# Macaron block (MoE, attention, MoE) on one core: attention output with tokens on partitions, layer 1's router begun inside the last attention steps, and two expert loads moved

## Chip, cores and metric

One core of a Trainium2 chip runs the whole program in one launch. The metric is the device time of that launch in microseconds (us). Engines: PE is TensorE, DVE is VectorE, ACT is ScalarE, POOL is GpSimd, SP is SyncE, which here only issues DMAs.

## What is computed

x has 8 x 256 = 2048 tokens of D = 256, float32. Two mixture-of-experts layers stand around one attention layer:

```python
x = x + 0.5 * moe(layernorm(x), router_w, w1, v1, w2)      # E = 64 experts, top K = 8, F = 96
x = x + attention(layernorm(x), Wq, bq, Wk, bk, Wv, bv, Wo, bo)  # H = 16 heads of 128, KV = 4
x = x + 0.5 * moe(layernorm(x), router_w, w1, v1, w2)

# moe: rows of tokens in order (position, batch); each expert keeps its first C = 32 tokens
probs = softmax(x @ router_w.T); wts, idx = top_k(probs, 8); wts = wts / sum(wts)
h = silu(xg @ w1) * (xg @ v1); y = h @ w2                  # xg: the 32 tokens of each expert
out[token] += weight * y
# attention: grouped queries, softmax(Q K^T / sqrt(128)) V per head, then @ Wo + bo
```

## The kernel before

**Layout.** x stays on chip as `x[128, 16, 256]`, token on partition, 16 tiles of 128 tokens. All engines run hand-written programs that meet at semaphores. PE, DVE, ACT and POOL each run theirs in order, so the order of the code is the order of the work.

**MoE layer.** PE transposes the token tiles (`transpose_tokens(layer, u)`, two tiles each, into PSUM bank u % 2), multiplies by the router (`experts_of`) and transposes the logits back (`logits_of`); ACT copies each result (`copy_tokens`, `copy_expert_major`, `copy_logits`). DVE takes the top eight of each token in four `masks(layer, n)` of four tiles each, with small operations of the layer norm (`moment_steps`) in between. PE packs the masks into codes (line 1338), DVE finds the first 32 tokens of each expert (`expert_layer` of DVE, lines 920 to 942), PE moves them to slots (line 1347, the slot product), and POOL gathers token rows from a table in DRAM by indirect DMA (line 552), one DMA for each of 16 groups of four experts. At most five gathers are in flight ahead. PE then walks the 16 groups (`slot_step`): transpose of the slots (line 1189), up product (1257), down product (1267), and one-hot products that sum into PSUM banks 5 to 7 (1201, 1217), which `take_tokens` has filled with x before (lines 1231 for 64 tokens of a tile, 1236 for 16 more). `keep_busy(n)` (line 1225) issues n matmuls whose result nobody uses; each shows as two in the profile, since a float32 matmul runs in two passes.

**Expert weights.** Group g needs 768 KB (up) and 512 KB (down). Homes for them share memory with other tensors: `q` (4 homes, over Wq, Wk, Wv), `r` (4, over attention's tensors), `o` (3, over Wo), `s` (1, over router tensors), and `r` again for groups 12 to 15. SP's program is one queue: in layer 1 it loads groups 0 to 3 during the last block of attention, 4 and 5 when attention is done, writes the token table (`store_table`), waits for two gathers, then loads 6 to 11, then 12 to 15 as homes come free. In layer 0, groups 4 to 11 follow the table at once, then 12 to 15, and behind them Wk, Wq, Wv, Wo.

**Attention.** Four blocks of 512 tokens (two sequences). Float32 products are made of three float32r products of high and low parts (`three`, lines 1406 to 1408). ACT takes the high part out of PSUM, DVE the low part (`take_high`, `take_low`), in two work banks used in turn; `work()` waits until the use before last was taken. A block has 16 steps, `place(n)` gives kv head, sequence bb and pair of heads hp. In `step(n)` of PE stand, in this order: scores of n+1, transposes of the probabilities of n, the first projection (`fills`: q each step, k in every fourth, xT and v near the block's end), the output products that are due, further projections, and the P·V product of n into a work bank, whose low part is o_lo. DVE's `step(n)`: maxima of n+1, probsT_lo, first projection, normalisation of probs n+1, other projections, o_lo, statistics (line 1150).

**Output.** `out_ps[d]` (banks 6 and 7) holds the output transposed: 128 columns of D on partitions, 512 tokens. In the first block up to step 12 `output_product` does one step: 12 matmuls of 256 columns. Later `output_of_pair` does two steps of a pair with one d at once: 6 matmuls of 512 columns. When a block is done ACT adds the bias on the way out (`take_output`, line 733), PE transposes it back (`transpose_output`, line 1506, in steps 2 and 3 of the next block, each in a work bank; `output`, line 1517, at the end), and DVE adds it to x (`add_output`, line 1103; `last_output`, line 1112):

```python
ps = work()
for t in range(4):
    last = nc.tensor.transpose(ps[:, t * P:t * P + P], yT[:, d, t * P:t * P + P], ident[:])
last.then_inc(y_ready, 1)
```

**From attention to layer 1.** The last step (15) already transposes tokens of tiles 0 to 3. Then, on PE: experts_of(1,0), tokens 2 and 3 (tiles 4 to 7), logits, last output product, experts 1, tokens 4 and 5, `output()`, and the rest. DVE does masks 0 with the moments of 12 tiles, the last add, its statistics, then masks 1 to 3.

## Time and profile before

| | us |
|---|---|
| median of 3 runs | 665.5 (663.27 to 667.88) |
| the profiled execution | 667.9 |
| its span, first to last instruction | 666.0 |
| PE busy | 626.7 |
| DVE busy | 498.3 |
| ACT busy | 391.1 |
| POOL busy | 52.4 |

The profile is of one execution, 2.4 us above the median. Busy times of PE overlap, since matmuls are pipelined: a matmul's duration is from its start to its modelled end, and the pace is read from the starts. PEclk is the share of full clock that TensorE was granted, 1.00 for 2.4 GHz, 0.50 for 1.2 GHz. In a timeline row "[0.48 <-DVE q_lo L1073]" means that the engine had been idle for 0.48 us until line 1073 released it.

### The profile page before, as it was taken

To read this page: it belongs to the slowest core of one execution; us is meant where nothing else is said; L and a number is where in the kernel's file an instruction comes from. 1 tells how busy PE (TensorE), PEld (TensorE's weight loads), DVE (VectorE), ACT (ScalarE), POOL (GpSimd) and SP (SyncE) were. 2 spreads that over 40 slices of the span, in tenths; PEclk is the share of its full clock that TensorE was granted. 3 is DMA by queue.
4 is the path that set the end of the run, shared out by engine and by line. 5 is a ranking of instruction groups with operands and counts; after the bars stand their busy time and mean duration, and the time that the engine had idled before them with its cause. 6 is when DMAs were issued, how large, how long until landed. Compare 5 with 4: busy or idle time off the path is not lost.

```text
span 666.0 us, 11671 instructions
## 1 busy us (share of the span) xinstructions
PE 626.7 (94%) x4320; PEld 525.8 (79%) x4320; DVE 498.3 (75%) x1309; ACT 391.1 (59%) x1053; POOL 52.4 (8%) x75
## 2 busy tenths in 40 slices
PE   8589999999999999999999999999999999887995
PEld 6367677999888888888888888888888888665774
DVE  6746668889988677887777788876778877773663
ACT  5634475767666566566556666666666656662441
POOL 3443000000000000000000000000000000134210
PEclk9689999999999999999999999999999999969998
DMA  8999940000000000000000000000000034266991
GB/s 318 341 416 419 376 153 1 2 1 1 0 1 1 1 1 0 1 1 1 0 1 1 1 0 1 1 1 0 1 1 2 0 127 190 110 207 228 419 376 48
DMA packets 27619, 62.50 MB, mean 94 GB/s; under 512 B 7014, under 2 KB 17382, under 8 KB 27558
## 3 DMA queue, kind: packets, MB, share of 16 engines
q1 hardware_dynamic: 25398, 55.97, 22.2%
q0 software_dynamic: 1664, 5.30, 2.1%
q8 instruction: 37, 0.61, 0.4%
q10 hardware_dynamic: 496, 0.43, 0.3%
q14 instruction: 24, 0.20, 0.1%
HBM read 54.34 MB, written 7.34 MB: 93 GB/s over the span
## 4 chain that ended last, share of the span: by engine, by line
PE 72%; DVE 12%; ACT 6%; DMA 6%; issue 2%; POOL 1%; SPq 0%; POOLq 0%; DVEq 0%; ACTq 0%
PE bank L1406 18%; PE bank L1408 17%; PE bank L1407 17%; PE bank L1462 7%; PE bank L1217 3%; DMA slots<-token_table,slot_index 3%; DMA down_r<-down_in 3%; PE bank L1257 2%; ACT probs L728 2%; PE bank L1225 2%; PE bank L1267 2%; ACT probsT_hi L739 1%; DVE q_lo L1073 1%; ACT q_hi L711 1%; DVE probsT_lo L1129 1%
## 5 line engine op out<-in xcount | busy, mean ns | idle before, releaser
L728 ACT ACTIVATE probs<-bank,negmax 128x256 f32<-128x256 f32 x256 | 121.4, 494 | 1.8 <-DVE negmax L1087 1.6
L739 ACT CAST probsT_hi<-bank 128x512 fp32r<-128x512 f32 x128 | 68.8, 590 | 70.9 <-PE bank L1462 70.9
L711 ACT ACTIVATE o_hi<-bank,bv 128x512 fp32r<-128x512 f32 x64 | 44.1, 690 | 69.2 <-PE bank L1408 69.2
L1129 DVE TENSOR_TENSOR probsT_lo<-bank,probsT_hi 128x512 fp32r<-128x512 f32 x128 | 81.7, 679 | 0.4 <-ACT probsT_hi L739 0.4
L1087 DVE TENSOR_REDUCE negmax<-bank 128x2 f32<-128x512 f32 x128 | 81.7, 679 | 0.0
L1095 DVE TENSOR_SCALAR probs<-probs,rowinv 128x256 f32<-128x256 f32 x256 | 73.0, 348 | 2.3
L1073 DVE SCALAR_TENSOR_TENSOR o_lo<-bank,bv,o_hi 128x512 fp32r<-128x512 f32 x64 | 48.0, 749 | 34.5 <-ACT o_hi L711 34.5
L1408 PE MATMUL bank<-k_hi,q_lo 128*128 128x256 f32 x256 | 72.4, 283 | 0.0
L1407 PE MATMUL bank<-k_lo,q_hi 128*128 128x256 f32 x256 | 72.3, 283 | 0.0
L1406 PE MATMUL bank<-k_hi,q_hi 128*128 128x256 f32 x256 | 72.2, 282 | 0.0
L1073 DVE SCALAR_TENSOR_TENSOR q_lo<-bank,bq,q_hi 128x512 fp32r<-128x512 f32 x64 | 47.9, 748 | 32.2 <-ACT q_hi L711 31.9
L1462 PE MATMUL bank<-ident,probs 128*128 128x128 f32 x512 | 66.4, 273 | 0.6 <-DVE probs L1095 0.6
L1462 PEld LDWEIGHTS bank<-ident,probs 128*128 128x128 f32 x512 | 57.3, 140 | 1.1 <-DVE probs L1095 1.1
L1406 PE MATMUL bank<-probsT_hi,v_hi 128*128 128x512 f32 x128 | 52.0, 406 | 6.1 <-DVE q_lo L1073 4.1
L728 ACT ACTIVATION_READ_ACCUMULATOR probs<-bank,negmax 128x1 f32 x256 | 57.6, 225 | 0.0
L1406 PE MATMUL bank<-o_hi,wo_hi 128*128 128x512 f32 (+1 forms) x160 | 56.6, 354 | 0.0
L1408 PE MATMUL bank<-o_hi,wo_lo 128*128 128x512 f32 (+1 forms) x160 | 55.7, 348 | 0.0
L1407 PE MATMUL bank<-o_lo,wo_hi 128*128 128x512 f32 (+1 forms) x160 | 55.4, 346 | 0.0
L1406 PE MATMUL bank<-xT_hi,wq_hi 128*128 128x512 f32 x128 | 54.3, 424 | 0.2 <-DVE k_lo L1073 0.2
L711 ACT ACTIVATE q_hi<-bank,bq 128x512 fp32r<-128x512 f32 x64 | 44.9, 702 | 15.0 <-PE bank L1408 15.0
L1406 PEld LDWEIGHTS bank<-k_hi,q_hi 128*128 128x128 f32 x256 | 48.7, 190 | 2.8 <-DVE q_lo L1073 0.3
L1407 PEld LDWEIGHTS bank<-k_lo,q_hi 128*128 128x128 f32 x256 | 48.7, 190 | 2.5
(184 smaller groups left out, 1294.9 us busy)
## 6 DMA issues: line engine op xcount, KB each, us to landing
up_r<-up_in SPq DMA_DIRECT2D x16, 768.0 KB, 9.3
down_r<-down_in SPq DMA_DIRECT2D x14, 512.0 KB, 11.1
up_q<-up_in SPq DMA_DIRECT2D x8, 768.0 KB, 8.8
up_o<-up_in SPq DMA_DIRECT2D x6, 768.0 KB, 14.6
down_q<-down_in SPq DMA_DIRECT2D x8, 512.0 KB, 9.6
token_table<-xn SPq DMA_DIRECT2D x16, 256.0 KB, 2.4
down_o<-down_in SPq DMA_DIRECT2D x6, 512.0 KB, 16.3
x<-x_in SPq DMA_DIRECT2D x4, 512.0 KB, 5.5
```

The source lines that it names most:

```text
L711: nc.scalar.activation(dst, src, ACT.Identity, bias=bias).then_inc(work_high, 1)
L728: nc.scalar.activation(probs[:, n % 2, t, :], scores_ps[head][:, qt * S:qt * S + S], ACT.Exp, bias=negmax[:, n % 2, t:t + 1], accum_out=ro ...
L739: nc.scalar.copy(probsT[0][:, head].rearrange("p c s -> p (c s)"), probsT_ps[head][:]).then_inc(probsT_high, 1)
L1073: nc.vector.scalar_tensor_tensor(lo, src, bias, hi.bitcast(f32), ALU.add, ALU.subtract).then_inc(work_taken, 1)
L1087: nc.vector.reduce_max(negmax[:, n % 2, 2 * head:2 * head + 2], scores_ps[head][:].rearrange("p (t s) -> p t s", t=2), AX.X, negate=True). ...
L1095: last = nc.vector.tensor_scalar(probs[:, n % 2, t, :], probs[:, n % 2, t, :], rowinv[:, n % 2, t:t + 1], None, ALU.mult)
L1129: nc.vector.tensor_tensor(probsT[1][:, head].rearrange("p c s -> p (c s)"), probsT_ps[head][:], probsT[0][:, head].rearrange("p c s -> p ( ...
L1217: last = mm(banks[n][:, D * pair:D * pair + D], marks[:, c:c + P], parts, start=start and pair == 0, stop=stop, skip_group_check=True)
L1406: mm(dst, w[0], m[0], start=start, stop=False, skip_group_check=shared)
L1407: mm(dst, w[0], m[1], start=False, stop=False, skip_group_check=shared)
L1408: return mm(dst, w[1], m[0], start=False, stop=stop, skip_group_check=shared)
L1462: last = nc.tensor.transpose(probsT_ps[head][:, c * S + qt * P:c * S + qt * P + P], probs[:, n % 2, 2 * head + qt, c * P:c * P + P], ident[:])
```

## The change

- `out_ps[bb]` now holds one sequence's output with tokens on partitions: the stationary operand is o (128 tokens), the moving one Wo (256 columns). Every product is that of the step before, 12 matmuls of 256 columns; o needs two homes instead of four, yT goes.
- ACT's `take_output` and PE's transposes go. DVE adds out_ps[bb] to x directly, sequence 0 in step 15, sequence 1 in step 1 of the next block.
- The bias is spread over partitions once, in layer 0 (ACT, PE, ACT), and DVE adds it to x in steps 13 and 14 of block 0 and 4 and 8 of the others.
- The product stands behind the first projection, in step 16 behind the second, and in step 12 half behind xT and half behind the last projection.
- Tokens of tiles 0 to 3 are transposed in step 14 of the last block, tiles 4 to 7 in step 15, with experts_of(1,0) ahead of that step's P·V; the moments of 12 tiles are in DVE's steps 11 and 12, the last add is inside masks 1.
- `take_tokens` for layer 1 is split: the wide part ahead of the codes, the narrow part behind them; 12 fillers instead of 16 stand before the slot product.
- SP loads groups 6 and 7 of layer 1 right behind the table and then waits for four gathers instead of two; in layer 0 it waits for the last expert load before it issues Wk.
- DVE's weight splits 6 to 9 come earlier in the first fills; one statistics operation moves from step 9 to 10.

```diff
-        SPREAD_AT = (5, 6, 7, 9)
+        SPREAD_AT = (5, 6, 7, 10)
+        BIAS_AT = ((13, 14), (4, 8))
@@ sync
-                for n in range(2):
+                for n in range(IN_FLIGHT - 1):
                     sp.wait_ge(gathered[n], 16 * (layer * len(range(n, GROUPS, RING)) + 1))
...
+            sp.wait_ge(home(0, GROUPS - 1)[2], 16 * loads_before(0, GROUPS - 1))
             sp.wait_ge(down_done, done_with_q)
...
             store_table(1)
+            for g in range(6, 8):
+                load(1, g)
             wait_for_gathers(1)
-            for g in range(6, AHEAD):
+            for g in range(8, AHEAD):
                 load(1, g)
@@ scalar, step
-                if i > 0 and n in (2, 3):
-                    act.wait_ge(y_raw, y_seen.add())
-                    take_output(n - 2)
...
                 if last and n == STEPS - 1:
-                    copy_tokens(0)
-                    copy_tokens(1)
+                    copy_tokens(2)
+                    copy_tokens(3)
+                    copy_expert_major(0)
...
+                if last and n == STEPS - 2:
+                    copy_tokens(0)
+                    copy_tokens(1)
@@ vector
-            in_fill = {1: 3, 2: 4, 3: 5, 4: 6, 6: 7, 7: 8, 8: 9}
+            in_fill = {1: [3], 2: [4], 3: [5], 4: [6, 7], 5: [8], 6: [9]}
...
+            def add_bias(i, bb):
+
+                xa = x[:, 4 * i + 2 * bb:4 * i + 2 * bb + 2, :]
+                nc.vector.tensor_tensor(xa, xa, bo_row[:].unsqueeze(1).to_broadcast([P, 2, D]), ALU.add).then_inc(bias_added, 1)
...
+                if i is not None and n in BIAS_AT[i > 0]:
+                    add_bias(i, BIAS_AT[i > 0].index(n))
+                if i is not None and n == 15:
+                    add_output(i, 0)
+                if i is not None and i > 0 and n == 1:
+                    add_output(i - 1, 1)
+                take_low(*[t[:, n % 2, :, :] for t in o], bv[:, kv:kv + 1])
+                if i is not None and i > 0 and n in SPREAD_AT:
+                    spread_of(i - 1, SPREAD_AT.index(n))
+                if last and n in (11, 12):
+                    for moment in steps_of_last[6 * (n - 11):6 * (n - 11) + 6]:
+                        moment()
...
+            masks(1, 0)
+            masks(1, 1, [lambda: None, last_output, lambda: spread_of(BLOCKS - 1, 2), lambda: tie(spread_of(BLOCKS - 1, 3))])
@@ tensor
+                if layer == 1:
+                    take_tokens()
...
-                take_tokens(layer)
-                if layer == 1:
-                    keep_busy(16)
...
+                if layer == 0:
+                    take_tokens()
+                else:
+                    take_narrow_tokens()
+                    keep_busy(12)
...
+                for qt in halves:
                     for head in range(2):
-                        last = three(out_ps[d][:, bb * S:bb * S + S], [a[:, G * kv + 2 * hp + head, d * P:d * P + P] for a in wo],
-                                     [a[:, home_of_o(n), head, :] for a in o], n % STEPS == 0 and head == 0,
-                                     n % STEPS == STEPS - 1 and head == 1, shared=True)
+                        h = G * kv + 2 * hp + head
+                        last = three(out_ps[bb][:, qt * D:qt * D + D], [a[:, n % 2, head, qt * P:qt * P + P] for a in o],
+                                     [a[:, h, :] for a in wo], hp == kv == qt == head == 0,
+                                     n in (13, 15) and qt == head == 1, shared=True)
...
-                if i > 0 and n in (2, 3):
-                    transpose_output(n - 2)
```

**Order on PE in step 3 of the second block**, from its last output product rows to P·V. Names are the tensors read; line 1506 transposes the output back. Before:

```order
L1406 MATMUL bank<-o_hi,wo_hi 128x512
L1407 MATMUL bank<-o_lo,wo_hi 128x512
L1408 MATMUL bank<-o_hi,wo_lo 128x512
L1506 MATMUL bank<-ident,yT 128x128 x4
L1406 MATMUL bank<-probsT_hi,v_hi 128x512
L1407 MATMUL bank<-probsT_lo,v_hi 128x512
L1408 MATMUL bank<-probsT_hi,v_lo 128x512
```

Changed, where lines 1404 to 1406 are the three products:

```order
L1404 MATMUL bank<-wo_hi,o_hi 128x256
L1405 MATMUL bank<-wo_lo,o_hi 128x256
L1406 MATMUL bank<-wo_hi,o_lo 128x256
L1404 MATMUL bank<-probsT_hi,v_hi 128x512
L1405 MATMUL bank<-probsT_lo,v_hi 128x512
L1406 MATMUL bank<-probsT_hi,v_lo 128x512
L1404 MATMUL bank<-probsT_hi,v_hi 128x512
```

The transposes are gone from between output product and P·V, and the product has 256 columns instead of 512.

**Order on PE at the end of the last step.** Line 1293 multiplies by the router, 1283 transposes tokens, 1304 transposes logits. Before, from the third row of the last P·V product:

```order
L1408 MATMUL bank<-probsT_hi,v_lo 128x512
L1406 MATMUL bank<-probsT_hi,v_hi 128x512
L1407 MATMUL bank<-probsT_lo,v_hi 128x512
L1408 MATMUL bank<-probsT_hi,v_lo 128x512
L1293 MATMUL bank<-xnT,router_w 64x256 x4
L1283 MATMUL bank<-ident,x 128x128 x8
L1304 MATMUL bank<-ident,logitsT 128x128 x2
L1406 MATMUL bank<-o_hi,wo_hi 128x256
L1407 MATMUL bank<-o_lo,wo_hi 128x256
L1408 MATMUL bank<-o_hi,wo_lo 128x256
```

Changed, from the last row of the output product of step 14; the router product, token and logits transposes are lines 1282, 1272 and 1293:

```order
L1406 MATMUL bank<-wo_hi,o_lo 128x256
L1282 MATMUL bank<-xnT,router_w 64x256 x4
L1404 MATMUL bank<-probsT_hi,v_hi 128x512
L1405 MATMUL bank<-probsT_lo,v_hi 128x512
L1406 MATMUL bank<-probsT_hi,v_lo 128x512
L1404 MATMUL bank<-probsT_hi,v_hi 128x512
L1405 MATMUL bank<-probsT_lo,v_hi 128x512
L1406 MATMUL bank<-probsT_hi,v_lo 128x512
L1293 MATMUL bank<-ident,logitsT 128x128 x2
L1282 MATMUL bank<-xnT,router_w 64x256 x4
L1272 MATMUL bank<-ident,x 128x128 x8
```

The first router product moved ahead of the last P·V, and the logits follow P·V at once.

**Order on PE between the last logits and the first slots.** Line 1338 makes the codes, 1231 and 1236 are the wide and the narrow token products, 1225 the fillers, 1347 the slot product. Before:

```order
L1304 MATMUL bank<-ident,logitsT 128x128 x2
L1338 MATMUL bank<-code_ident,chosen 128x128 x8
L1231 MATMUL bank<-x,ident 64x256 x8
L1236 MATMUL bank<-x,moved_ident 128x256 x8
L1225 MATMUL bank<-router_w,ident 128x128 x16
L1347 MATMUL bank<-ident,slot_keys 32x16 x4
L1225 MATMUL bank<-router_w,ident 128x128 x16
```

Changed (codes 1329, wide 1218, narrow 1225, fillers 1212, slot product 1345):

```order
L1293 MATMUL bank<-ident,logitsT 128x128 x2
L1218 MATMUL bank<-x,ident 64x256 x8
L1329 MATMUL bank<-code_ident,chosen 128x128 x8
L1225 MATMUL bank<-x,moved_ident 128x256 x8
L1212 MATMUL bank<-router_w,ident 128x128 x12
L1345 MATMUL bank<-ident,slot_keys 32x16 x4
L1212 MATMUL bank<-router_w,ident 128x128 x16
```

The wide token products went ahead of the codes, and four fillers fewer stand in front of the slot product.

## Rows read from the trace of the kernel before

**Rows 1.** The page, part 1: busy us (share of the span) x instructions.

```profile
PE 626.7 (94%) x4320; PEld 525.8 (79%) x4320; DVE 498.3 (75%) x1309; ACT 391.1 (59%) x1053; POOL 52.4 (8%) x75
```

**Rows 2.** Timeline of PE, first score products of steps: start us, us, engine, line, op.

```profile
122.56 0.28 PE L1406 MATMUL bank<-k_hi,q_hi 128*128 128x256 f32 x1
129.09 0.28 PE L1406 MATMUL bank<-k_hi,q_hi 128*128 128x256 f32 x1
...
238.30 0.28 PE L1406 MATMUL bank<-k_hi,q_hi 128*128 128x256 f32 x1
...
245.90 0.28 PE L1406 MATMUL bank<-k_hi,q_hi 128*128 128x256 f32 x1
...
261.30 0.28 PE L1406 MATMUL bank<-k_hi,q_hi 128*128 128x256 f32 x1
...
267.74 0.28 PE L1406 MATMUL bank<-k_hi,q_hi 128*128 128x256 f32 x1
...
553.14 0.28 PE L1406 MATMUL bank<-k_hi,q_hi 128*128 128x256 f32 x1
...
558.75 0.28 PE L1406 MATMUL bank<-k_hi,q_hi 128*128 128x256 f32 x1
```

**Rows 3.** Groups by line and form, PE: x count, busy us, mean ns, idle before.

```profile
L1406 PE MATMUL bank<-o_hi,wo_hi 128*128 128x512 f32 x96 | 38.1, 396 | 0.0
```

**Rows 4.** Waits of PE: us in total, times, longest us.

```profile
PE bank L1189 <- DMA slots<-token_table,slot_index: 6.1, 4, 3.5
...
PE bank L1406 <- DVE q_lo L1073: 4.4, 11, 0.5
PE bank L1406 <- DVE k_lo L1073: 2.2, 6, 1.0
...
PE bank L1257 <- DMA down_r<-down_in: 0.8, 1, 0.8
```

**Rows 5.** Timeline of DVE, end of attention to the last keys.

```profile
570.71 0.75 DVE L1073 SCALAR_TENSOR_TENSOR o_lo<-bank,bv,o_hi 128x512 fp32r<-128x512 f32 x1 [2.95 <-ACT o_hi L711]
...
583.62 0.43 DVE L910 TENSOR_TENSOR chosen<-struck,logits 128x256 fp32r<-128x256 f32 x1
...
585.58 0.43 DVE L910 TENSOR_TENSOR chosen<-struck,logits 128x256 fp32r<-128x256 f32 x1
...
596.02 0.42 DVE L939 MAX8 slot_keys<-merged 64x8 f32<-64x256 f32 x1
```

**Rows 6.** Chain that ended last, in order of time: start us, us, what.

```profile
587.17 3.41 PE bank L1231 x16
590.58 4.07 PE bank L1236 x16
594.66 6.57 PE bank L1225 x32
...
605.82 7.15 DMA slots<-token_table,slot_index
...
615.40 0.62 PE bank L1189 x2
...
619.29 0.37 PE bank L1189 x2
...
622.17 0.37 PE bank L1189 x2
```

**Rows 7.** Timeline of PE, 16 fillers behind the slot product, layer 0 and layer 1.

```profile
31.51 6.58 PE L1225 MATMUL bank<-router_w,ident 128*128 128x128 f32 x32
...
601.34 3.84 PE L1225 MATMUL bank<-router_w,ident 128*128 128x128 f32 x32
```

**Rows 8.** The tile slots: us from a gather's issue to its landing.

```profile
DMA to landing us min/median/max: 2.9/6.3/7.1
```

**Rows 9.** Windows: length, busy of each engine (x), PEclk, DMA share, GB/s.

```profile
76.00:77.00 1.00, 1.00 (x26) 0.68 (x24) 0.90 (x4) 0.29 (x2) 0.00 (x0) 1.00 1.04 264
615.00:616.00 1.00, 1.00 (x7) 0.67 (x4) 0.13 (x1) 0.47 (x1) 0.00 (x0) 0.50 1.04 421
```

More of the change, by code:

```diff
@@ L1509, in output @@
-            def output():
-                pe.wait_ge(yT_ready, yT_seen.add(KD))
-                for pair in range(2):
-                    ps = work()
-                    for t in range(2):
-                        for d in range(KD):
-                            c = (2 * pair + t) * P
-                            last = nc.tensor.transpose(ps[:, t * D + d * P:t * D + d * P + P], yT[:, d, c:c + P], ident[:])
-                    last.then_inc(y_ready, 1)
+                        h = G * kv + 2 * hp + head
@@ L1545, in step @@
                 last_use[("o", n % STEPS)] = uses[0]
+                if last and n == STEPS - 2:
+                    pe.wait_ge(exp_ready, exp_seen.add(4))
+                    for u in range(2):
+                        transpose_tokens(1, u)
             xn4_seen.add(4)
```

189 lines of the change are left out of this document (74 added, 115 removed).

## The prediction

> **What bounds the kernel now.** I read the page first: TensorE is busy for 94% of the span [rows 1], so a microsecond of work on it in the attention stage is a microsecond of time. Then the timeline of TensorE, step by step. A step is the stretch from the first score product (k_hi,q_hi) of one head pair to that of the next. With one projection in it, it takes 129.09 - 122.56 = 6.53 us in the first block, where output products are 256 columns wide, and 267.74 - 261.30 = 6.44 us in later blocks, where they are 512 wide [rows 2]. Steps 2 and 3 of each later block, which transpose the projected output back, take 245.90 - 238.30 = 7.60 us [rows 2]. A step with neither projection nor transposes takes 558.75 - 553.14 = 5.61 us [rows 2]: there TensorE waits in a loop, P·V product, o_hi on ScalarE, o_lo, maxima and probsT_lo on VectorE, next P·V.
>
> Behind attention the rule changes. From 570.7 to 613 TensorE works mostly to fill time. The end is set by VectorE's chain of masks and keys [rows 5], by TensorE's own queue in front of the slot product, and by the gathers [rows 6]. Its keys are ready at 596.02 + 0.42 = 596.4, yet the slot product starts at 601.2, because 4.07 us of narrow token products and 6.57 us of idle-filling matmuls stand in front of it in program order [rows 5, 6].
>
> **The change, part by part.**
>
> *Output products, +4.3 us.* 96 matmuls of each of three kinds have 512 columns [rows 3], six matmuls to a step's worth, so 48 of them; each becomes 12 of 256 columns and costs 6.53 - 6.44 = 0.09 us more [rows 2]: 48 x 0.09 = 4.3. The Trainium skill, "TensorE: Matmul & The Clock Gate", section Back-to-back issue gap, gives N/2.4 + 2.5 ns for one matmul; by that two of 256 cost 2.5 ns more than one of 512, and 288 pairs 0.7 us, which would put the end 3.6 us earlier. The row is 15 ns for a pair, and the row decides.
>
> *Output transposes, -7.0 us.* The six steps with them take 7.60 instead of 6.44, 1.16 each, of which 0.45 to 0.5 is the wait for q_lo behind them, since they take a work bank of their own [rows 2, 4]. Both go: -7.0. ScalarE loses eight 128x512 evictions, which cost nothing. VectorE's adds number eight as before, and eight adds of the bias of about 0.68 us each are new. They stand ahead of o_lo, where VectorE waits some 0.6 us for o_hi in most steps, in long steps (4, 8, 14) or in step 13 of the first block. I take 0, and up to 5.4 if nothing covers them.
>
> *Places in the steps, -3.3 us.* Step 16 of three blocks waits about 0.5 us for q_lo; with the product behind the second projection that wait has 1.4 us of cover: -1.5. Moving one set of statistics from step 9, which also normalises tokens, to step 10 gives about -0.35 twice. Step 12 gets half a product at its end but only half between xT and k: xT_lo is then late for k's second half by 0.65 where k_lo was late by 0.45; I take +0.4 for three. Two steps' products leave the last block for steps 13 and 14 of the first, which had none and waited about 0.5 us each: -0.8. In the first fills the longest wait for k_lo, 1.0 us [rows 4], follows two weight splits that now come earlier: -0.7. Sum -3.65; since each is a small wait replaced by another, I count -3.3.
>
> *Moments inside steps 11 and 12 of the last block, +2.4 us.* Eleven dependent levels of about 0.2 us stand right behind o_lo, in the loop that sets the 5.61 us step. Nothing hides them: 1.4 in step 12 and 1.0 in step 13.
>
> *Router inside the last steps, -2.1 us.* In step 15 the two token copies on ScalarE delay probsT_hi by 0.45 and the expert product (1.0 us) is now ahead of P·V: o_lo ends about 1.1 later than 571.46. VectorE then needed 586.01 - 571.46 = 14.55 us to the last mask [rows 5]. Now: no wait for the first logits; shifts 0.2; two statistics 0.7; four masks at 585.58 - 583.62 = 1.96 each, 7.8; the last add 0.65; two more statistics 0.7; the moments of four tiles interleaved, about 1.2. Together 11.3, so -3.2. With +1.1 the masks and all behind them come 2.1 earlier.
>
> *TensorE's queue before the slot product, -4.7 us.* The wide products, 3.4 us [rows 6], move ahead of the code products, where TensorE had waited for masks, and the fillers drop from 16 to 12. Behind the codes stand then 4.1 + 12 x 0.41 (6.57 / 16) = 9.0 us, and VectorE's keys take 596.44 - 587.2 = 9.2: keys decide. 601.2 - 596.4 = 4.8; less a signal, 4.7. The slot product starts near 594.4, with attention left where it was.
>
> *Gathers and loads, -1.8 us.* What is late next: 16 fillers, which took 3.84 us in layer 1 and 6.58 us in layer 0, where TensorE had idled before the slot product as it now will [rows 7], and the first gather with the seventh and eighth load in its way. A gather lands after 2.9 us at best, 6.3 median, 7.1 at most [rows 8]. The fillers end near 601.1, the gather lands between 598.1 and 602.2; the first slot is transposed near 601.1, 6.7 us behind the slot product instead of 3.8: +2.9. In return the fourth gather, 7.15 us in the chain now [rows 6], has no six loads beside it, and TensorE's longest wait for slots, 3.5 us [rows 4], goes: -3.5. Behind that wait the granted clock was 0.50, 1.2 GHz [rows 9], and one slot took 619.29 - 615.40 = 3.89 instead of 622.17 - 619.29 = 2.88 [rows 6]: -1.2 with the piece before it. The loads now held for four gathers are groups 8 to 11, wanted 15 us later, 5.2 MB at some 0.4 MB/us: 13 us. They fit.
> The Trainium skill, "DMA: Bandwidth & Descriptors", section Queues, rings and completion order, says that each DMA engine takes turns between its queues packet by packet. By that the gather waits for its share and not for the whole of both loads, and would land near the lower end, with the fillers deciding; the 7.15 us row beside a full queue shows that the share can be small.
>
> *Layer 0, -0.3 us.* SyncE now waits for the last expert load before it issues the projection weights. While both were in flight the engines moved 264 GB/s at a share of 1.04 [rows 9], against over 400 otherwise, and TensorE waited 0.8 us for that load [rows 4]. Alone the load should land about 1.5 us earlier, and the projection weights about 0.7 later; ScalarE splits them in program order ahead of the last groups' evictions, so a late wk would hold those. Bounds: -0.8, and +3.0 if the load lands no earlier and each weight a round trip later. I take -0.3. The bias row (two activations, two products, one copy) lies under waits of ScalarE and TensorE.
>
> Sum: +4.3 - 7.0 - 3.3 + 2.4 - 2.1 - 4.7 - 1.8 - 0.3 = -12.5 us. The profiled execution took 667.9 (span 666.0 and 1.9 around it), 2.4 above the median of 665.5. So 655.4 on its scale, 653.0 on the median's.
>
> **Rivals.**
>
> *A better tail, 649.5.* If the wide products and the codes keep the clock up, the fillers take 3.8 us and the gather decides at 2.9 to 3.5: 2.7 less; with layer 0 at -0.8 it is 3.5 less. For it: those products fill idle time. Against: layer 0, the same pattern, was at half clock.
>
> *The transfers hit back, 658.5.* Layer 0 at its bound (+3.3), the first gather at 7.1 us (+1.1) and the second again behind it (+1.1). For it: 7.15 beside queued loads. Against: two loads are 2.6 MB, gone some 6.5 us after they start.
>
> *VectorE becomes the bound, 659.* The eight bias adds cost their 5.4 us and the product waits for o_lo about 0.6 more. For it: VectorE is busy 5.4 us in a step of 6.44. Against: the first block made its products in the very order of the new one and kept 6.53. By this rule the time is about that of no change.
>
> *The clock falls for the whole slot loop, 669.* If TensorE idles long enough before slot 0 and the clock stays at 0.50 through the loop, each of 16 slots costs 3.89 instead of 2.88: +16.2, slower than before. It decides from about 13 slots at half clock on. Against: layer 0 starts its loop after the same idle time and runs at full clock from the first slot.
>
> **How the numbers follow.** Forecast 60%, better tail 16%, transfers 12%, VectorE 9%, clock 3%. A measurement of this kernel tells about 1% from no change, 6.7 us: 658.8 and 672.2. The first two and half of the third are faster by more than that, with some doubt of all small terms: 0.89. The rest of the third and the fourth are within 1%: 0.08. Slower 0.03. The range reaches from 648, a little past the better tail, to 660, which takes in both rivals near 659.
>
> **What would show it.** Right: steps 2 and 3 of later blocks at about 6.5 us; all plain steps 6.53; steps 12 and 13 of the last block near 7.0 and 6.6; no wait of TensorE for the fourth gather; slot product within 0.5 us of the last keys; that product near 590.5 (601.2 less 3.9 up to the end of attention, 2.1 and 4.7). Wrong: bias adds followed by TensorE waits for o_lo; ScalarE waiting at wk's split at 80 us; slots of 3.9 us; a first gather over 7 us.

## The result, and the profile after

The changed kernel takes 660.47 us (median of 8 runs, 658.23 to 661.30) against 667.27 us for the kernel before on the same chip (median of 8 runs, one of which took 2100 us; 667.07 without it): ratio 0.991, 95% interval 0.9888 to 0.9932, so 4.5 to 7.5 us faster. The forecast was 653.0 with a range of 648 to 660. The direction is right, the size is about half, and the median lies 0.5 us outside the range. The gain is also at the edge of the 1% that the prediction set as what can be told from no change: the medians of this set differ by 1.0%, the ratio by 0.9%.

The profiled execution took 658.23 us, the shortest of the eight, with a span of 656.4 us. Its page, part 1, against [rows 1]:

```profile
PE 621.8 (95%) x4572; PEld 536.4 (82%) x4572; DVE 503.5 (77%) x1316; ACT 386.0 (59%) x1048; POOL 51.9 (8%) x75
```

PE is busy 5 us less and has 252 matmuls more (288 for the halved width, 4 for the bias row, less 32 transposes and 8 passes of fillers). The output products are now groups of 256 columns, for the 96 of 512 in [rows 3]. Groups of the page, part 5, and the bias adds:

```profile
L1404 PE MATMUL bank<-wo_hi,o_hi 128*128 128x256 f32 x256 | 73.1, 286 | 0.0
...
L1084 DVE TENSOR_TENSOR x<-x,bo_row 128x512 f32<-128x512 f32 x8 | 5.5, 682 | 0.0
```

**Attention.** Timeline of PE, first score products of steps, as in [rows 2]:

```profile
100.63 0.28 PE L1404 MATMUL bank<-k_hi,q_hi 128*128 128x256 f32 x1
...
240.53 0.28 PE L1404 MATMUL bank<-k_hi,q_hi 128*128 128x256 f32 x1
247.06 0.28 PE L1404 MATMUL bank<-k_hi,q_hi 128*128 128x256 f32 x1
...
542.38 0.28 PE L1404 MATMUL bank<-k_hi,q_hi 128*128 128x256 f32 x1
549.37 0.28 PE L1404 MATMUL bank<-k_hi,q_hi 128*128 128x256 f32 x1
555.88 0.28 PE L1404 MATMUL bank<-k_hi,q_hi 128*128 128x256 f32 x1
```

Step 2 of the second block takes 247.06 - 240.53 = 6.53 us where it took 7.60 [rows 2]. Steps 12 and 13 of the last block take 6.99 and 6.51 with the moments in them. But the first row stands 1.4 us later than the 99.21 of the kernel before.

**Waits.** Waits of all engines: us in total, times, longest; to hold beside [rows 4]:

```profile
PE bank L1176 <- DMA slots<-token_table,slot_index: 5.6, 4, 3.2
...
ACT wo_hi L677 <- DMA wo_raw<-wo_in: 2.2, 1, 2.2
PE bank L1256 <- ACT hiddenT L566: 1.8, 2, 1.4
...
ACT wk_hi L677 <- DMA wk_raw<-wk_in: 1.2, 1, 1.2
...
PE bank L1404 <- DVE q_lo L1055: 0.2, 1, 0.2
```

The waits for q_lo are down from 4.4 to 0.2 us and the one for down_r is gone. In their place ScalarE waits for wk and wo. The 5.6 us for slots are nearly the 6.1 of before, and their longest is now the first gather's.

**Behind attention.** Timeline of VectorE, as in [rows 5]: last o_lo, last mask, a cast, last keys.

```profile
569.08 0.75 DVE L1055 SCALAR_TENSOR_TENSOR o_lo<-bank,bv,o_hi 128x512 fp32r<-128x512 f32 x1 [3.33 <-ACT o_hi L703]
...
580.43 0.42 DVE L892 TENSOR_TENSOR chosen<-struck,logits 128x256 fp32r<-128x256 f32 x1
...
586.01 1.23 DVE L909 CAST best_rank<-best 128x32 int32<-128x32 f32 x1
...
591.40 0.42 DVE L921 MAX8 slot_keys<-merged 64x8 f32<-64x256 f32 x1
```

Timeline of PE from the narrow products to the second slot, for [rows 6, 7]:

```profile
581.51 4.89 PE L1225 MATMUL bank<-x,moved_ident 16*128 16x256 f32 x16
586.32 5.03 PE L1212 MATMUL bank<-router_w,ident 128*128 128x128 f32 x24
591.88 0.25 PE L1345 MATMUL bank<-ident,slot_keys 64*32 64x16 f32 x8 [0.53 <-DVE slot_keys L921]
592.06 3.84 PE L1212 MATMUL bank<-router_w,ident 128*128 128x128 f32 x32
599.06 0.44 PE L1176 MATMUL bank<-ident,slots 128*128 128x128 f32 x2 [3.17 <-DMA slots<-token_table,slot_index]
600.47 0.41 PE L1176 MATMUL bank<-ident,slots 128*128 128x128 f32 x2 [0.96 <-DMA slots<-token_table,slot_index]
600.80 1.41 PE L1246 MATMUL bank<-up_q,slotsT 128*32 128x192 f32 x16
```

The slot product now starts on the keys, 591.88 instead of 601.16. Then TensorE waits 3.17 us for the first gather. GpSimd issues it at 592.72, and VectorE, which waits for it too, goes on at 599.04, 6.3 us later. The kernel before had 7.15 us for its fourth [rows 6]. Timelines of GpSimd and VectorE:

```profile
592.72 0.99 POOL L536 DMA_INDIRECT slots<-token_table,slot_index  x1 [5.52 <-DVE slot_index L929]
...
599.04 0.22 DVE L848 TENSOR_REDUCE total<-slots 128x1 f32<-128x64 f32 x1 [6.18 <-DMA slots<-token_table,slot_index]
```

Windows of that stretch, columns as in [rows 9]:

```profile
588.00:590.00 2.00, 2.00 (x11) 2.00 (x11) 1.85 (x7) 0.61 (x2) 0.00 (x0) 0.50 1.10 340
...
596.00:598.00 2.00, 0.00 (x0) 0.00 (x0) 0.00 (x0) 0.00 (x0) 1.39 (x3) 1.00 1.00 402
...
602.00:604.00 2.00, 2.00 (x20) 1.08 (x20) 1.32 (x8) 0.87 (x3) 0.00 (x0) 0.50 0.79 230
```

PE is idle and the DMA engines are full with the seventh and eighth load. Behind that idle time the granted clock is 0.50, the 1.2 GHz level, and the up products of a slot take 1.41 us instead of the 0.86 they take from 605 us on. The half clock of [rows 9] is still there; it has moved from the fourth slot to the products of the first two and the transposes of the third.

### The profile page after: what moved, and what is told of

It is laid out like the page before. It is cut to its first block, busy times and chain, and to the rows that moved or that the text cites. A ratio compares the mean times of both kernels' runs of the same rounds, so it can differ in the third digit from the quotient of the medians.

```text
span 656.4 us, 12187 instructions
## 1 busy us (share of the span) xinstructions
PE 621.8 (95%) x4572; PEld 536.4 (82%) x4572; DVE 503.5 (77%) x1316; ACT 386.0 (59%) x1048; POOL 51.9 (8%) x75
## 4 chain that ended last, share of the span: by engine, by line
PE 79%; DVE 11%; DMA 6%; ACT 2%; issue 1%; POOL 0%; POOLq 0%; SPq 0%; DVEq 0%
PE bank L1404 20%; PE bank L1406 19%; PE bank L1405 19%; PE bank L1460 8%; PE bank L1246 4%; PE bank L1204 4%; DMA slots<-token_table,slot_index 3%; DMA wo_raw<-wo_in 2%; PE bank L1256 2%; PE bank L1176 2%; DVE probsT_lo L1104 1%; DVE negmax L1069 1%; PE bank L1272 1%; DVE ln L809 1%; DVE struck L888 1%
## 5 line engine op out<-in xcount | busy, mean ns | idle before, releaser
L1404 PE MATMUL bank<-wo_hi,o_hi 128*128 128x256 f32 x256 | 73.1, 286 | 0.0
L1406 PE MATMUL bank<-wo_hi,o_lo 128*128 128x256 f32 x256 | 72.6, 284 | 0.0
L1405 PE MATMUL bank<-wo_lo,o_hi 128*128 128x256 f32 x256 | 72.3, 282 | 0.0
L720 ACT ACTIVATION_READ_ACCUMULATOR probs<-bank,negmax 128x1 f32 x256 | 57.8, 226 | 0.0
L703 ACT ACTIVATE q_hi<-bank,bq 128x512 fp32r<-128x512 f32 x64 | 45.0, 703 | 12.5 <-PE bank L1406 12.5
```

What stands on the lines that cost most here:

```text
L703: nc.scalar.activation(dst, src, ACT.Identity, bias=bias).then_inc(work_high, 1)
L720: nc.scalar.activation(probs[:, n % 2, t, :], scores_ps[head][:, qt * S:qt * S + S], ACT.Exp, bias=negmax[:, n % 2, t:t + 1], accum_out=ro ...
L1404: mm(dst, w[0], m[0], start=start, stop=False, skip_group_check=shared)
L1405: mm(dst, w[0], m[1], start=False, stop=False, skip_group_check=shared)
L1406: return mm(dst, w[1], m[0], start=False, stop=stop, skip_group_check=shared)
```

## The experiments

Sixteen kernels ran, the two unaltered ones among them. Ratios are to the kernel before, on the same chip; a recorded ratio and the quotient of two medians differ by up to 0.2%.

**e3: the changed kernel again.** No edit.

> The changed kernel once more, unaltered, to see what differs between its executions: the first profile took 658.2 us, the median of its runs was 660.5. Theory (the clock behind the gathers' wait): typical executions spend longer at half clock between the first mask and the third slot, near 585 and 600 us, which gives 2 us; the attention steps keep 6.53 us. Rival: the 2 us lie spread over the attention stage, where single steps take longer.

Measured: 659.78 us, ratio 0.9902 (0.988 to 0.9925). The stage from the first score product of attention to that of the last step takes 455.27 us against 455.25: nothing varies there. The spans differ by 1.5 us; 1.1 of it stands between the last keys and the slot product, and 0.6 in the slot loop, where the granted clock is 0.50 from 600 to 606. Timeline of PE of e3:

```profile
581.65 6.37 PE L1225 MATMUL bank<-x,moved_ident 16*128 16x256 f32 x16
587.96 5.22 PE L1212 MATMUL bank<-router_w,ident 128*128 128x128 f32 x24
593.11 0.25 PE L1345 MATMUL bank<-ident,slot_keys 64*32 64x16 f32 x8
```

A window of each, first the changed kernel's first profile, then e3:

```profile
590.00:592.00 2.00, 1.48 (x17) 1.28 (x16) 1.72 (x6) 0.00 (x0) 0.00 (x0) 0.82 0.89 223
```
```profile
590.00:592.00 2.00, 2.00 (x12) 2.00 (x11) 1.83 (x7) 0.00 (x0) 0.00 (x0) 0.50 0.96 234
```

Narrow products and 12 fillers take 11.5 us here and 9.8 in the first profile, where the granted clock had risen to 0.82 by then. No wait for keys is left: the last keys end at 591.97, and TensorE's queue starts the slot product 1.14 us behind them. The theory holds in kind, with 1.5 us for its 2; the moment at which the clock changes is worth over 1 us.

**e13: the kernel before again.** No edit.

> The kernel before, unaltered, for a second profile. Theory (the first profiled execution, 667.9 us, was 1 to 2 us slower than usual in parts that the change does not touch): attention starts near 98.5 instead of 99.2 us, the stage between first score products of first and last step keeps 459.5 us, and the time is 665.5 to 666.5. Rival: all segments repeat within 0.3 us.

Measured: ratio 0.9993 (0.9971 to 1.0015); span 664.7 us against 666.0. Neither text was right: attention starts at 99.38, the stage keeps its length (459.40 against 459.54), and the 1.3 us is in TensorE's queue again: keys to slot product 3.40 us instead of 4.72.

One thing differs that the forecast had built on. The 3.5 us wait for the fourth gather [rows 4] is not there; the longest wait for a gather is 1.2 us. Yet the fourth slot is transposed 5.6 us behind the third (5.5 in the first profile), because ScalarE stops instead. Timeline of ScalarE in e13:

```profile
608.71 0.25 ACT L588 ACTIVATE gate<-bank 128x96 f32<-128x96 f32 x1 [2.78 <-remote]
```

Two profiles of each kernel give this ledger, in us. The stretches are read from the timelines; the forecast is split at the same places.

| stretch | before, e13 | changed, e3 | change of the means | forecast |
|---|---|---|---|---|
| to the first score product | 99.21, 99.38 | 100.63, 100.74 | +1.4 | -0.3 |
| to the last step's | 459.54, 459.40 | 455.25, 455.27 | -4.2 | -3.6 |
| to the end of o_lo | 12.71, 12.71 | 13.95, 13.96 | +1.2 | +1.1 |
| to the last mask | 14.55, 14.54 | 11.02, 11.03 | -3.5 | -3.2 |
| to the last keys | 10.43, 10.44 | 10.97, 10.97 | +0.5 | 0 |
| to the slot product | 4.72, 3.40 | 0.06, 1.14 | -3.5 | -4.7 |
| to the first slot | 3.85, 3.86 | 7.18, 6.96 | +3.2 | +2.9 |
| to PE's last matmul | 54.06, 54.04 | 50.29, 50.88 | -3.5 | -4.7 |

The sum is -8.3 before rounding, with the end -8.2.

**e1: without the wait in layer 0.**

```diff
-            sp.wait_ge(home(0, GROUPS - 1)[2], 16 * loads_before(0, GROUPS - 1))
             sp.wait_ge(down_done, done_with_q)
```

> The changed kernel without SyncE's wait for layer 0's last expert load ahead of the projection weights. Theory (the wait delays Wk and Wo): Wk is issued near 63 us as before the change instead of at 78, ScalarE no longer waits 1.2 us for wk and 2.2 us for wo, and the first score product moves from 100.6 back to about 99.2 us; time 1.4 us below the changed kernel, about 659.0, ratio to the kernel before 0.988 to 0.989. Rival (the wait pays for itself): TensorE's 0.8 us wait for down_r at 79 us returns and the first score product stays at 100.6; time 660.5 as the changed kernel. Second rival (the bias row costs it): wk lands early, yet the start of attention stays 1.4 us late because of the added activations and products.

Measured: 658.09 us, ratio 0.9867 (0.9844 to 0.9889), 1.7 us below e3 in the same set. Timeline of SyncE, and of PE, in e1:

```profile
63.79 0.41 SPq L434 DMA_DIRECT2D wk_raw<-wk_in  x1
```
```profile
99.42 0.28 PE L1403 MATMUL bank<-k_hi,q_hi 128*128 128x256 f32 x1
```

Timelines of SyncE, ScalarE and PE in the changed kernel, where the wait holds Wk until 78.03 us:

```profile
78.03 0.41 SPq L435 DMA_DIRECT2D wk_raw<-wk_in  x1
...
81.92 0.63 ACT L677 ACTIVATE wk_hi<-wk_raw 128x512 fp32r<-128x512 f32 x1 [1.22 <-DMA wk_raw<-wk_in]
...
82.75 0.42 PE L1256 MATMUL bank<-down_r,hiddenT 96*32 96x256 f32 x4 [1.44 <-ACT hiddenT L566]
...
95.18 0.63 ACT L677 ACTIVATE wo_hi<-wo_raw 128x512 fp32r<-128x512 f32 x1 [2.24 <-DMA wo_raw<-wo_in]
```

Over all profiles with the changed layer 0, attention starts between 100.1 and 101.1 us (eight), and without the wait between 97.9 and 99.4 (e1, e11, e12, e16), as in the kernel before and the kernels made from it with its layer 0 (98.2 to 99.4, five). So the wait costs 1.2 us between this profile and the first of the changed kernel, and 1.9 between the means of the eight and the five. Without it ScalarE waits for neither weight, and the 0.8 us wait for down_r does not return. So the theory of the late weights stands, and neither contention nor the bias row costs what was lost. The wait for down_r varies by itself: it is 0.6 to 0.8 us in four of the five profiles with the old layer 0 and absent in e5.

**e15: that wait alone, in the kernel before.**

> The kernel before with one part of the change alone: SyncE's wait for layer 0's last expert load ahead of the projection weights. Theory (late Wk and Wo): TensorE's 0.8 us wait for down_r goes, ScalarE waits some 1.2 us for wk and 2.2 us for wo, and the first score product comes 1.5 to 2 us later; ratio 1.002 to 1.003. Rival (it costs only beside the bias row of the changed kernel): no later start, ratio 1.000 or below.

Measured: ratio 1.0025 (1.0001 to 1.0048), +1.7 us, or +2.6 by the medians. The first score product comes at 102.10 us, 2.7 us or more behind the five profiles without the wait, where 1.5 to 2 were expected, and ScalarE waits 1.2 us for wk and 3.2 for wo. The wait costs by itself, though the interval ends just above 1.

**e4: the queue in front of the slot product alone.**

```diff
+                if layer == 1:
+                    take_tokens()
...
-                take_tokens(layer)
-                if layer == 1:
-                    keep_busy(16)
+                if layer == 0:
+                    take_tokens()
+                else:
+                    take_narrow_tokens()
+                    keep_busy(12)
```

> The kernel before with one part of the change alone: layer 1's wide token products ahead of its code products and 12 fillers instead of 16 behind the narrow ones. Theory (TensorE's queue held the slot product): the slot product starts within 0.5 us of the last keys, 4.7 us earlier (near 596.4 on the first profile's scale), the 16 fillers behind it stay at full clock with 3.8 us, and the first slot follows at 3.8 us as before; time 4.7 us below the kernel before, 662.6, ratio 0.993. Rival (the clock): TensorE idles ahead of the slot product, the fillers run at half clock in 6.6 us and the fourth gather meets the same loads; gain 1.9 us, ratio 0.997.

Measured: 664.17 us against 666.96, ratio 0.9956 (0.9934 to 0.9978), -2.9 us. Timeline of PE:

```profile
586.06 6.61 PE L1238 MATMUL bank<-x,moved_ident 16*128 16x256 f32 x16
592.60 4.99 PE L1225 MATMUL bank<-router_w,ident 128*128 128x128 f32 x24
597.52 0.25 PE L1353 MATMUL bank<-ident,slot_keys 64*32 64x16 f32 x8
597.71 3.84 PE L1225 MATMUL bank<-router_w,ident 128*128 128x128 f32 x32
```

The keys ended at 595.83: the queue is still 1.7 us late. The fillers behind keep full clock, so the rival fails, but the forecast's price of the queue fails too: 592.60 - 586.06 for the narrow products and 597.52 - 592.60 for the fillers, 11.5 us and not 9.0.

**e14: the loads alone, in the kernel before.** Groups 6 and 7 behind the table, four gathers ahead of the rest.

> The kernel before with one part of the change alone: layer 1's seventh and eighth load right behind its table, and four gathers instead of two ahead of the other loads. Theory (the part is worth something alone, where the slot product comes at 601 us and both loads have landed by then, and loses it in the whole change, where the slot product comes at 592 beside them): first gather at 2.9 us as before, no 3.5 us wait for the fourth gather, time 3 to 4.5 us below the kernel before, ratio 0.994. Rival (the gathers are slow whatever stands beside them): time within 1 us of the kernel before.

Measured: ratio 1.0003 (0.9979 to 1.0028). No gain, though the longest wait of TensorE for a gather is 1.2 us instead of 3.5 (two waits, 2.1 us in all). The profiled execution is the slowest of its twelve. Two things stand in it in the place of the wait. In this execution the clock stayed at 0.50 until 602, and the slot product came 7.6 us behind the keys. Then ScalarE stood still. Timeline of ScalarE in e14:

```profile
612.57 0.25 ACT L590 ACTIVATE gate<-bank 128x96 f32<-128x96 f32 x1 [3.56 <-remote]
```

The up products that this row needs ended at 609.4. What it waited for has no name in the profile. The repeat of the kernel before (e13) has the same stop with 2.78 us and no long wait for a gather either, so the 3.5 us were not there to be won in every execution.

**e2: the loads back behind the gathers, in the changed kernel.**

```diff
-            for g in range(6, 8):
-                load(1, g)
             wait_for_gathers(1)
-            for g in range(8, AHEAD):
+            for g in range(6, AHEAD):
```

> The changed kernel with the seventh and eighth load put back behind the wait for the gathers (four of them, where the kernel before waited for two). Theory (two loads in flight slow the first gathers): the first gather lands 2.9 us after its issue instead of 6.3, TensorE goes from the 16 fillers straight into slot 0 near 596 instead of 599.1, stays at full clock, and the fourth gather lands with nothing beside it; time 3 us below the changed kernel, about 657.5. Rival (the stall only moves): with six loads starting behind the fourth gather, the fifth and sixth gathers take 7 us, TensorE waits some 3 us for a slot and runs one slot at half clock; time 660 to 661 as the changed kernel.

Measured: 657.65 us, ratio 0.9866 (0.9843 to 0.9888), 2.1 us below e3. The first slot is transposed 3.86 us behind the slot product, for 7.18: both loads in flight did cost 3.3 us. Of it 1.6 is left at PE's last matmul (55.84 us behind the slot product, for 57.47). The rest is lost around a stop like that of e14; that the stop costs it is not shown by a run. Timeline of ScalarE in e2:

```profile
600.01 0.25 ACT L570 ACTIVATE gate<-bank 128x96 f32<-128x96 f32 x1 [2.11 <-remote]
```

**e8: more fillers ahead of slot 0.**

```diff
-                keep_busy(16)
+                keep_busy(16 if layer == 0 else 28)
```

> The changed kernel with 28 instead of 16 idle-filling matmul pairs between layer 1's slot product and slot 0 (3.8 + 2.9 us at full clock, up to the landing of the first gather). Theory (idle TensorE loses the clock): slots 0 to 2 run at full clock instead of half, the up products of 1.4 us become 0.86, the third slot's transposes come 1.5 to 2 us earlier behind the first slot's, and the time falls by about 1.5 us to 658.5. Rival (the gathers set the pace of slots 0 to 3): the clock is full but TensorE waits for gathers instead, and the time stays at 660.

Measured: 656.37 us, ratio 0.9873 (0.9853 to 0.9893). Timeline of PE, and one window:

```profile
592.31 6.52 PE L1212 MATMUL bank<-router_w,ident 128*128 128x128 f32 x56
599.12 0.44 PE L1176 MATMUL bank<-ident,slots 128*128 128x128 f32 x2 [0.29 <-DMA slots<-token_table,slot_index]
...
601.01 0.86 PE L1246 MATMUL bank<-up_q,slotsT 128*32 128x192 f32 x16
```
```profile
602.00:604.00 2.00, 1.76 (x29) 0.86 (x27) 1.64 (x9) 1.07 (x4) 0.00 (x0) 1.00 0.80 199
```

The first slot comes when it did, the granted clock is 1.00 instead of 0.50, the up products take 0.86 us, and from slot product to PE's last matmul it is 56.22 us instead of 57.47. In the six profiles with 16 fillers behind the slot product and the loads in flight this stretch takes 56.7 to 57.8 us. Work that computes nothing saves about 1 us by keeping the clock.

**e10: 6 fillers ahead, 28 behind.** One edit more: `keep_busy(12)` becomes `keep_busy(6)`.

> The changed kernel with 6 instead of 12 fillers ahead of the slot product and 28 instead of 16 behind it. Theory (at half clock the narrow products take 6.4 us and 12 fillers 4.9, more than the keys' 10.3, so in most executions TensorE's queue and not the keys starts the slot product): the slot product starts within 0.1 us of the keys in every profile, 1.1 us earlier than in the repeat of the changed kernel, and the time is 0.5 to 1 us below that with 28 fillers alone, about 655.7. Rival (TensorE's idle time there loses the clock again): the 28 fillers run at half clock, end some 4 us after the first gather, and the time is 660 or more.

Measured: 658.82 us, ratio 0.9876 (0.9848 to 0.9904), like e8. The slot product stands on the keys (0.06 us), but the fillers behind it begin at half clock (0.50 at 594 to 596) and the last of them starts at 599.5, while the first gather has landed by 598.7. What the queue gives, the clock takes.

**e5: the kernel before with 256-wide output matmuls.** Each `three(sums, ...)` of a pair becomes two, one per sequence.

> The kernel before with each 512-wide matmul of the output products cut into two of 256 columns with the same weights, nothing else changed (288 matmuls become 576). Theory of the forecast: each of the 48 products costs 0.09 us more, the one-projection steps of later blocks go from 6.44 to 6.53 us, and the time rises by 4.3 us, ratio 1.006. Rival, by the fixed cost per matmul that the Trainium skill (TensorE: Matmul & The Clock Gate, section Back-to-back issue gap) gives: 0.7 us in all, ratio 1.001. Second rival: the steps of 6.53 in the first block are that long for another reason than the width, and nothing changes here.

Measured: ratio 1.0048 (1.0027 to 1.0069), +3.2 us; the stage of attention takes 462.51 us instead of 459.54, +3.0. Plain steps go from 6.44 to 6.53 as forecast, but steps 2 and 3 stay at 7.61 and step 12 changes by 0.05: there the product lay under a wait. The 0.7 us that the fixed cost per matmul in the Trainium skill gives (TensorE: Matmul & The Clock Gate, section Back-to-back issue gap) are too few by this run.

**e6: the moments back into the masks.** The loop over `steps_of_last` leaves `step`; `masks(1, 0, steps_of_last)` runs them.

> The changed kernel with the moments of the first twelve tiles taken out of steps 11 and 12 of the last block and put back into the first masks behind attention. Theory of the forecast: steps 12 and 13 of the last block shorten by 1.4 and 1.0 us to 5.6 us each, o_lo ends 2.4 us earlier, and the masks take 2.4 to 3 us longer: time within 1 us of the changed kernel, 659 to 661. Rival (the moments lie beside other work in the masks): the masks take at most 1 us longer and the time falls by 1.5 us or more.

Measured: 659.75 us, ratio 0.9914 (0.9899 to 0.9928), as the changed kernel. Steps 12 and 13 take 5.63 and 5.61 us, 2.3 less together, and the masks 12.29 instead of 11.02: between the two texts, and 1.0 us to the good at the keys. In its profile TensorE's queue, 1.18 us late, took that back at the slot product.

**e7: no bias adds.** It leaves out adding the output bias.

> The changed kernel without the eight adds of the output bias on VectorE (the output lacks that bias). Theory of the forecast: they lie in VectorE's idle time ahead of o_lo; steps 4, 8 and 14 keep their lengths and the time stays at the changed kernel's 660. Rival (VectorE is the bound): each add costs its 0.68 us, the steps that hold one shorten by it, and the time falls by up to 5.4 us, to 655.

Measured: 659.52 us, ratio 0.9907 (0.9893 to 0.9922). Every step keeps its length within 0.02 us. The adds cost nothing.

**e9: GpSimd's products in pieces.**

```diff
-                    nc.gpsimd.tensor_tensor(expw[:, 8 * h:8 * h + 8, :], ...
+                    for q in range(0, 8, 2):
+                        last = nc.gpsimd.tensor_tensor(expw[:, 8 * h + q:8 * h + q + 2, :], ...
```

> The changed kernel with GpSimd's two 128x512 products of expert weights and masks each cut into four of 128x128. In the changed kernel VectorE's cast best_rank takes 1.2 us beside the second of them and 0.2 us elsewhere. Theory (the cast is held until the GpSimd instruction ends; the Trainium skill, SBUF — State Buffer, describes such an exclusive lock of a port pair): the cast takes at most 0.5 us, the last keys come 0.7 to 1.0 us earlier behind the last mask (10.2 us instead of 10.97), and the time falls by at most that, to a ratio of 0.989 to 0.990, because TensorE's fillers may then hold the slot product. Rival (the long cast has another cause): it stays at 1.2 us.

Measured: ratio 0.9902 (0.9872 to 0.9932), no change. Timeline of VectorE in e9:

```profile
585.98 0.43 DVE L911 CAST best_rank<-best 128x32 int32<-128x32 f32 x1
586.32 0.49 DVE L912 TENSOR_SCALAR best_code<-best 128x32 int32<-128x32 f32 x1
586.85 0.49 DVE L913 TENSOR_TENSOR part_bits<-best_code,bit_of_part 128x128 int32<-128x128 int32 x1
```

The cast falls from 1.23 to 0.43 us, so GpSimd's instruction did hold it. But in the changed kernel the next two take 0.17 and 0.29 us, and GpSimd's product itself grows from 2.50 to 3.45 us: the wait was spread, and the keys end 11.10 us behind the last mask for 10.97.

**e11, e12, e16: together.** e11 is the changed kernel with the edits of e1, e9 and e10.

> The changed kernel without SyncE's wait in layer 0, with GpSimd's products in pieces, 6 fillers ahead of and 28 behind the slot product. If the causes add: -1.6 (layer 0), -2.5 (clock), -0.5 to -1.5 (keys and queue): 654 to 655, ratio 0.981 to 0.983. If they cover each other: 656, no better than with 28 fillers alone.

Measured: 657.04 us, ratio 0.9852 (0.9825 to 0.9879). The parts do not add: the time is above both texts, and the ratio is 0.002 below that of the 28 fillers alone (e8), which is about what layer 0's part gives (1.4 us). The two intervals overlap.

> As the kernel with all three, but the seventh and eighth load behind the wait for four gathers, 16 fillers ahead of slot 0 and 4 more ahead of slots 0 and 1. Theory (the loads delay the first gather, and the idle gaps between the first slots lose the clock): the first slot comes 3 us earlier behind the slot product, the clock stays full through slots 0 to 3, and the time is 1 to 2 us below the kernel with all three, 653. Rival (gathers at one per 1.3 us and VectorE's part of a slot set the pace of the first four slots): time equal to the kernel with all three or 1 us above.

Measured: 655.62 us, ratio 0.9836 (0.9809 to 0.9863). Window of e12, columns as before:

```profile
598.00:600.00 2.00, 1.80 (x16) 1.25 (x17) 0.56 (x4) 0.78 (x3) 0.00 (x0) 1.00 0.81 252
```

It is 1.4 us below e11, as the theory had it, though not at 653. The first slot comes 6.39 us behind the slot product, 2.0 and not 3 us sooner than in e11 (8.40), since the 16 fillers in front of it take 6.32 us, near half clock. The clock stays full through the first slots, although ScalarE stands for 2.4 us there too.

> The kernel of e12 with GpSimd's two products whole again and 10 instead of 6 fillers ahead of the slot product. Theory (cutting them only spread VectorE's wait): time equal to e12 within 0.5 us, ratio 0.983 to 0.985. Rival: the pieces were worth 0.7 us or more, ratio 0.985 or above.

Measured: 656.49 us, ratio 0.9835 (0.9801 to 0.9869). By this pair the pieces were worth nothing, though e16 also has 10 fillers in front of the slot product instead of 6. In e16 the clock does fall: it is 0.50 at 602 to 604, behind a stop of ScalarE of 2.6 us, so the four fillers ahead of slots 0 and 1 do not keep it every time. e12 and e16 are the fastest, some 4 us below the changed kernel.

## Why the prediction was right in direction and wrong in size

Of the 5.7 us between -12.5 and the -6.8 of the medians, 4.3 are in terms of the sum (-12.5 against the ledger's -8.2). The rest is between profiles and medians. No single wrong mechanism stands behind the 4.3: three terms were mis-sized, each by 1.2 to 1.7 us.

**Right.** Output products and transposes, places and moments: -4.2 for -3.6. The width cost 3.0 instead of 4.3, since 0.09 us was charged to steps where the product lay under a wait (e5); the transposes gave 6 x (7.61 - 6.53) = 6.5 for 7.0; the moments cost 2.3 for 2.4 (e6). What is left for the places is 3.0 for 3.3, as a remainder and not by a run of its own. The step lengths, with the width in them, go the way that was forecast: the first step of attention 9.44 to 8.66, step 16 of three blocks 9.72 to 9.26, step 10 of two 6.86 to 6.53, step 12 of three 8.81 to 8.99. Router: o_lo 1.2 late for 1.1, masks 11.0 us long for 11.3. The bias adds are free (e7), so VectorE did not become the bound. The clock does not stay at half for the whole slot loop.

**Wrong: layer 0, "-0.3 us", measured +1.4 in the ledger, +1.9 over all profiles.** The step that failed is "Alone the load should land about 1.5 us earlier, and the projection weights about 0.7 later". TensorE's wait for down_r went, but one of 1.44 us for hiddenT came in its place, because ScalarE splits wk ahead of that eviction and wk was late. The mechanism stood in the prediction as a bound and as a sign of being wrong (ScalarE waiting at wk's split); I took the value near the other end. Shown by e1 (-1.7 us when undone) and e15 (+1.7 us alone).

**Wrong: TensorE's queue, "-4.7 us", measured -3.5.** The step was "4.1 + 12 x 0.41 = 9.0 us ... keys decide". The 4.07 us for the narrow products in [rows 6] were at nearly full clock, while the fillers were priced near half. Windows of the kernel before over these two stretches, columns as in [rows 9], give 0.93 and 0.54:

```profile
590.00:594.00 4.00, 4.00 (x19) 2.99 (x16) 3.71 (x14) 3.21 (x6) 1.82 (x2) 0.93 0.94 292
594.00:601.00 7.00, 7.00 (x34) 6.42 (x32) 2.27 (x8) 0.00 (x0) 0.00 (x0) 0.54 0.19 43
```

Near half clock the narrow ones take 6.4 to 6.6 us (e3, e4), the queue 11.5, and in such executions it decides and not the keys. One row was used outside the clock in which it was measured.

**Wrong: gathers and loads, "-1.8 us", measured -0.3.** The first part held: the first slot 7.0 to 7.2 us behind the slot product for 6.7. There the fillers did keep full clock and the gather decided, the opposite of what was assumed, at almost the same price. The page DMA: Bandwidth & Descriptors of the Trainium skill (section Queues, rings and completion order) says that a DMA engine takes turns between its queues packet by packet; the early landing that I drew from it is not borne out: 6.3 us beside two loads, 2.9 without (e2). Most of the delay, 2.4 of 3.4 us, is ahead of the gather's data and not between its packets: from the issue at 592.7 to 596.8 no packet of its queue moves in the changed kernel, while in e2 they begin 1.7 us behind the issue. The second part is the step that failed: "TensorE's longest wait for slots, 3.5 us [rows 4], goes: -3.5", with "-1.2" for the clock; the two gave 3.5 together. A wait as long, 3.2 us, now stands ahead of the first gather, and the clock falls there: the idle time put the products of slots 0 and 1 at half clock; e8 shows that by filling it. And the 3.5 us was read from one profile: in the four others that issue these loads as before, the longest wait for a gather is 1.2 to 2.1 us (e13, e15, e4, e5), and in all of them but e5 ScalarE's stop stands there instead.

**Not priced: +0.5.** The keys took 0.5 us more. The cast best_rank fell beside GpSimd's product and took 1.23 us for 0.25, +1.0; it had stood at the product's end before. Another 0.45 came back ahead of it: the first operation on the keys starts 0.8 us behind the last mask instead of 1.3, since the code products ran at a higher clock (0.66 us for 1.11).

**Slips in the prediction's sums.** The places add up to -3.3 as listed, not to -3.65, so nothing was taken off for small waits that replace others. The better tail is 2.7 + 0.5 = 3.2 us less, 649.8 and not 649.5. The chances do not follow from the list: by its own rule more than 1% faster gets 0.60 + 0.16 + 0.06 = 0.82 and within 1% 0.15, for the 0.89 and 0.08 given.

**The base.** I took 2.4 us off for the profiled execution of before, from three runs. Over all sets the median of before is 666.0 to 667.3, so that execution was 0.6 to 1.9 high. The same -12.5 from 667 is 654.5, and the range moved with it, 649.5 to 661.5, would have held the 660.47. The base decides whether the range holds; it does not make the size right. About 1 us between the ledger's -8.2 and the -6.8 and -7.2 of the medians stays unassigned; the two profiled executions of the changed kernel took 658.2 and 659.7 us, 1.2 below the medians of their sets on average.

Alone, the parts measured -2.9 (queue, e4), +3.2 (width, e5), 0 (loads, e14) and +1.7 (layer 0, e15), forecast at -4.7, +4.3, -1.8 and -0.3: each that was tried alone came out less favourable than forecast, but for the width. The transposes, the places and the router were not tried alone.

## What to carry to other kernels

Price each instruction from a row at the clock it will run at, and write that clock beside the row: two rows from one stretch can stand at different levels. When a stall is removed from a chain whose clock falls with idle time, ask where the idle time goes; the half clock moves with it, and a few matmuls that compute nothing can win it back (about 1 us here, e8). A wait that guards one transfer delays all that its queue issues behind it: look first for an engine that takes these in program order ahead of what the critical path needs.

## What was not expected of the hardware

- ScalarE stood 2.1 to 3.6 us at the first slots with a releaser that the profile calls remote in e2, e4, e12, e13, e14, e15 and e16, all with no load beside the first gathers, and in no profile where loads 6 and 7 were in flight. The first profile of before and e5 had no load either and no such stop. In e2 it stands where half of the 3.3 us gained is lost again. No run settles what it is.
- A GpSimd product of 1.25 us held a VectorE cast of 0.25 us until it ended (1.23 us); cut into four (e9), it held each of the next instructions a little, to nearly the same sum.
- The moment at which the clock falls and returns differs by 1 us and more between executions of one kernel, and the start of attention scatters as much between kernels that differ little up to there (97.9 to 99.4 us without the wait), while the time between the first score product and the last step's repeats within 0.02 us in the changed kernel and 0.14 in the kernel before.
